# Front of a gated delta-rule layer: squares summed in column tiles, norms one visit later, clip and mask on GpSimd

## What is computed

```python
qkv = jax.nn.silu(_causal_conv1d(qkv, conv_weight))      # 4 taps
...
q = _l2norm(q) * Dk ** (-0.5)                            # x * rsqrt(sum(x * x) + 1e-6)
k = _l2norm(k)
...
g = jnp.cumsum(g.reshape(Bq, H, nc, chunk_size), axis=-1)
decay_mask = jnp.exp(jnp.clip(g[..., :, None] - g[..., None, :], -30.0, 30.0))
decay_mask = decay_mask * jnp.tril(jnp.ones((chunk_size, chunk_size), jnp.float32))
attn = -(jnp.einsum('bhcid,bhcjd->bhcij', k_beta, k) * decay_mask)
attn = jnp.where(upper, 0.0, attn)
...
qk = jnp.einsum('bhid,bhjd->bhij', q_c, k_c)
intra = jnp.where(mask_upper1, 0.0, qk * dm_c)
```

## Time and profile before

| What | Value |
|---|---|
| three runs | 4242.19, 4244.93, 4248.18 us (median 4244.93) |
| profiled execution | 4242.88 us, of it span 4241.1 us |
| mean granted TensorE clock | 0.953 |
| TensorE busy | 3878.7 us, 91% |
| VectorE busy | 2586.0 us, 61% |
| ScalarE busy | 2192.8 us, 52% |
| GpSimd busy | 942.5 us, 22% |
| the stage `delta_front` | about 1383 to 1887 us |

### The profile page before, as it was taken

One profiled execution on the slowest core, in us unless ns is written; L12 is line 12 of the kernel. 1 busy time (PEld: TensorE's weight loads), 2 busy tenths in 40 slices (PEclk: granted clock), 3 DMA queues, 4 the chain that ended last, 5 costly groups with the idle time before them and its releaser, 6 DMA issues. The chain is left out here.

```text
span 4241.1 us, 74265 instructions
## 1 busy us (share of the span) xinstructions
PE 3878.7 (91%) x25346; PEld 2809.3 (66%) x25346; DVE 2586.0 (61%) x7005; ACT 2192.8 (52%) x5801; POOL 942.5 (22%) x849
## 2 busy tenths in 40 slices
PE   7989889899895899979999999999999999978778
PEld 4555545555553666658888888888888888854444
DVE  4753467787523789966666666666666666532632
ACT  3741256676312566655665666666666666632122
POOL 0010010000000344543233323323322323311311
PEclk9999989998996999989999999999999999979879
DMA  2010100000100666553333333333333333222002
GB/s 79 1 35 0 49 1 2 2 2 2 33 0 22 195 229 221 204 195 89 84 84 95 82 91 95 94 81 93 90 78 93 87 82 85 70 81 77 24 28 91
DMA packets 443155, 322.90 MB, mean 76 GB/s; under 512 B 330208, under 2 KB 380064, under 8 KB 440736
## 3 DMA queue, kind: packets, MB, share of 16 engines
q1 hardware_dynamic: 439712, 309.75, 25.4%
q0 software_dynamic: 3072, 8.39, 0.6%
HBM read 200.13 MB, written 117.88 MB: 75 GB/s over the span
## 5 line engine op out<-in xcount | busy, mean ns | idle before, releaser
L2414 ACT ACTIVATE d_heads_VP<-d_heads_chain,d_GALL 128x128 f32<-128x128 f32 x512 | 188.6, 368 | 632.7 <-PE d_heads_chain L2308 629.6
L2557 DVE SCALAR_TENSOR_TENSOR d_heads_S<-d_heads_S,d_GALL,d_heads_chain 128x128 f32<-128x128 f32 x768 | 232.8, 345 | 381.0 <-PE d_heads_chain L2315 379.1
L616 ACT ACTIVATE b_heads_PR<-b_heads_sc,b_heads_NM 128x384 f32<-128x384 f32 (+3 forms) x512 | 272.9, 535 | 161.5 <-DVE b_heads_NM L684 161.5
L2493 POOL TENSOR_TENSOR d_heads_KD<-d_heads_KR,d_GALL 128x512 f32<-128x512 f32 x256 | 269.7, 1074 | 283.9 <-ACT d_heads_KR L2382 283.9
L2194 PE MATMUL d_heads_value<-all_XT,d_heads_WVZ 128*128 128x256 f32 x1024 | 292.5, 389 | 19.2 <-POOL d_heads_ZS L2472 19.2
L2339 PE MATMUL d_heads_projected<-d_heads_WO,d_heads_OT 128*128 128x256 f32 x1024 | 288.4, 394 | 20.1 <-ACT d_heads_OT L2433 19.8
L1981 DVE SCALAR_TENSOR_TENSOR d_front_CY<-d_front_proj,d_CW,d_front_CY 128x511 f32<-128x511 f32 (+2 forms) x384 | 271.8, 744 | 49.8 <-ACT d_front_CY L1892 45.3
L2535 DVE SCALAR_TENSOR_TENSOR d_heads_CY<-d_heads_value,d_CW,d_heads_CY 128x511 f32<-128x511 f32 (+2 forms) x384 | 283.2, 742 | 22.1 <-ACT d_heads_CY L2375 22.0
L2216 PE MATMUL d_heads_value<-d_heads_WVZ,all_XT 128*128 128x256 f32 x1024 | 284.6, 380 | 1.3 <-DVE d_heads_CY L2535 1.3
L2315 PEld LDWEIGHTS d_heads_chain<-d_heads_VP,d_heads_KD 128*128 128x128 f32 x1792 | 264.1, 191 | 29.9 <-ACT d_heads_VP L2414 9.1
L2315 PE MATMUL d_heads_chain<-d_heads_VP,d_heads_KD 128*128 128x128 f32 x1792 | 277.6, 277 | 5.5 <-ACT d_heads_VP L2414 5.5
(11 more groups left out here) (348 smaller groups left out, 8937.3 us busy)
## 6 DMA issues: line engine op xcount, KB each, us to landing
d_kq<-d_front_KQ SPq DMA_DIRECT2D x64, 768.0 KB, 5.0
d_heads_KQ<-d_kq SPq DMA_DIRECT2D x64, 768.0 KB, 4.9
d_heads_GE<-d_gerows SPq DMA_DIRECT2D x128, 256.0 KB, 5.2
d_front_GR<-d_grows SPq DMA_DIRECT2D x32, 512.0 KB, 6.5
d_it<-d_front_LI SPq DMA_DIRECT2D x64, 256.0 KB, 2.1
d_l<-d_front_LI SPq DMA_DIRECT2D x64, 256.0 KB, 3.9
d_heads_ITB<-d_it SPq DMA_DIRECT2D x128, 128.0 KB, 2.9
d_heads_WVZ<-w_d_qkvz SPq DMA_DIRECT2D x32, 256.0 KB, 6.5
```

The costliest lines, as they stand in the source:

```text
L616: nc.scalar.activation(PR[p % 3][j][:, 0:width(p)], SC[p % 2][j][:, 0:width(p)], ACT.Exp, bias=NM[:, u % 2, t, slot:slot + 1], scale=-1.0 ...
L2493: nc.gpsimd.tensor_tensor(KD[i % 2][:, 4 * q:4 * q + 4, h, :], KR[q][:, :, :], decay, ALU.mult).then_inc(kds, 1)
L2557: stt(S[:, h, :], S[:, h, :], gate(i, GEL0 + h, c), R[h][:, HD:2 * HD], ALU.mult, ALU.add).then_inc(su, 1)
```

## The change

- `lengths` is split. `square_rows(i)` makes the column of ones the weights (128x32) and the squares the moving side: four matmuls, for two chunks each, write to four ranges of 32 partitions of SSQ, 256 columns wide. Each row of a range then holds the sums of its two chunks. ScalarE copies this 128x256 block to RW (`copy_rows`), and the new `lengths(i)` turns it with two matmuls: RW's halves as weights, four columns of the identity as the moving side. Both come one visit later than the squares.
- `norms(g - 1)` runs in visit b = 0 of the next group; the root of a group on GpSimd and the store of the scaled products (`store_l`, now b = 2) follow it.
- Clip and mask go from VectorE to GpSimd, as four maxima and four additions a group. `scale` stands between them, `root` behind.
- The scratch tile TMP of the inversion lies in XN, a tile of the whole program.

```diff
-        ones = s.sb("ones", [P, 1])
+        ones = s.sb("ones", [P, HB])
...
+        RW = [s.sb(f"RW{r}", [P, 2, P]) for r in range(2)]
...
-        INV, TO, TMP = s.sb("INV", [P, HB, HB]), s.sb("TO", [P, HB, HB]), s.sb("TMP", [P, HB * HB // 4])
+        INV, TO, TMP = s.sb("INV", [P, HB, HB]), s.sb("TO", [P, HB, HB]), XN[:, 0, :]
...
-                if b == 1 and g >= 1:
+                if b == 2 and g >= 1:
                     store_l(g - 1)
...
+            def square_rows(i):
+                pe.wait_ge(squares, i + 1)
+                if i >= 1:
+                    pe.wait_ge(rowc, i)
+                if i % BATCH == 0 and i > 0:
+                    pe.wait_ge(kss, i)
+                for q in range(4):
+                    mm = nc.tensor.matmul(SSQ[q * HB:(q + 1) * HB, 0:2 * P], ones[:, :],
+                                          SQ[i % 2][:, 2 * q:2 * q + 2, :, :].rearrange("p c k n -> p (c k n)"),
+                                          start=True, stop=True)
+                mm.then_inc(srow, 1)
+
             def lengths(i):
                 g, b = divmod(i, BATCH)
-                pe.wait_ge(squares, i + 1)
-                if b == 0 and g >= 1:
-                    pe.wait_ge(kss, 4 * g)
-                for c in range(NCH):
-                    at = (g % 2) * 32 + b * NCH + c
-                    mm = nc.tensor.matmul(SSQ[:, at:at + 1], SQ[i % 2][:, c, :, :].rearrange("p k n -> p (k n)"),
-                                          ones[:, :], start=True, stop=True)
+                pe.wait_ge(rowc, i + 1)
+                for m in range(2):
+                    at = 2 * P + (g % 2) * 32 + b * NCH + m
+                    mm = nc.tensor.matmul(SSQ[:, at:at + NCH - 1:2], RW[i % 2][:, m, :], C.ident[:, 0:P:HB],
+                                          start=True, stop=True)
                 mm.then_inc(ssq, 1)
...
             for i in range(VISITS):
                 if i + 1 < VISITS:
                     project_keys(i + 1)
+                if i >= 1:
+                    square_rows(i - 1)
                 products(i)
-                lengths(i)
+                if i >= 1:
+                    lengths(i - 1)
+            square_rows(VISITS - 1)
+            lengths(VISITS - 1)
...
+            def copy_rows(i):
+                act.wait_ge(srow, i + 1)
+                if i >= 2:
+                    act.wait_ge(ssq, i - 1)
+                nc.scalar.copy(RW[i % 2][:, :, :], SSQ[:, 0:2 * P].rearrange("p (m n) -> p m n", m=2)).then_inc(rowc, 1)
+
             def exponential(g):
-                act.wait_ge(clips, BATCH * (g + 1))
+                act.wait_ge(hides, BATCH * (g + 1))
...
+                if i >= 1:
+                    copy_rows(i - 1)
                 act.wait_ge(silus, 2 * i + 2)
                 if i >= 2:
-                    act.wait_ge(ssq, i - 1)
+                    act.wait_ge(srow, i - 1)
...
+            copy_rows(VISITS - 1)
...
+            pool.wait_ge(const, 16)
...
+                for b in range(BATCH):
+                    pool.wait_ge(args, BATCH * g + b + 1)
+                    nc.gpsimd.tensor_scalar(D[g % 2][:, b], D[g % 2][:, b], -30.0, None, ALU.max).then_inc(clips, 1)
+
+            def hidden(g):
+                for b in range(BATCH):
+                    pool.wait_ge(clips, BATCH * g + b + 1)
+                    nc.gpsimd.tensor_tensor(D[g % 2][:, b], D[g % 2][:, b], hide[:, :].unsqueeze(1).broadcast_to([P, NCH, CHUNK]),
+                                            ALU.add).then_inc(hides, 1)
...
             exponents(0)
+            hidden(0)
             for g in range(HK):
+                if g + 1 < HK:
+                    exponents(g + 1)
                 if g >= 1:
                     scale(g - 1)
                 if g + 1 < HK:
-                    exponents(g + 1)
+                    hidden(g + 1)
+                if g >= 1:
+                    root(g - 1)
                 if g == 4:
                     pool.wait_ge(invl, 256)
                     nc.gpsimd.memset(INV[:, :, :].rearrange("p a n -> p (a n)")[:, 0:HB * HB:HB + 1], 1.0).then_inc(diag, 1)
-                root(g)
             scale(HK - 1)
+            root(HK - 1)
...
-            def clip(g, b):
-                dve.wait_ge(args, BATCH * g + b + 1)
-                stt(D[g % 2][:, b], D[g % 2][:, b], -30.0, hide[:, :].unsqueeze(1).broadcast_to([P, NCH, CHUNK]),
-                    ALU.max, ALU.add).then_inc(clips, 1)
...
-            for b in range(BATCH):
-                clip(0, b)
             conv(0)
             for i in range(VISITS):
                 g, b = divmod(i, BATCH)
                 if i + 1 < VISITS:
                     conv(i + 1)
                 decayed(i)
-                if b in (1, 2) and g + 1 < HK:
-                    clip(g + 1, 2 * b - 2)
-                    clip(g + 1, 2 * b - 1)
-                if b == 3:
-                    norms(g)
+                if b == 0 and g >= 1:
+                    norms(g - 1)
...
+            norms(HK - 1)
```

12 lines of the change are left out of this document (6 added, 6 removed).

## The result

| | before | changed |
|---|---|---|
| median of 6 runs each, same chip | 4241.85 us | 4231.57 us |
| lowest and highest | 4240.06, 4248.18 | 4225.14, 4233.75 |
| profiled execution (span) | 4242.88 (4241.1) | 4231.71 (4229.9) |

The ratio is 0.997, its 95% interval 0.9957 to 0.9983: faster by 0.3%, 10.3 us, a little more than the 0.2% that can be told from no change.

What follows compares the result with a forecast made beforehand. TensorE was taken as the bound, VectorE close behind, with a ScalarE loop in each fourth visit. Terms -11.2 - 1.5 + 3.5 - 1 = -10.2 us made 4232.7 profiled, 4234.7 as median; forecast 4234, range 4220 to 4254.

Steps and rivals of the forecast that it cites:

- plain groups: Groups without inversion steps, about 8 of 16: TensorE-bound, -1.4 us each with copy and norms wait, -11.2 in all.
- Part 1: Squares on TensorE: 1.80 us a visit becomes 0.69 for column sums plus 0.45 for turning; visit 7.21 to 6.55.
- Parts 2 and 3: ScalarE's new copy adds 0.30 us a group; norms a visit later make TensorE wait about 1.0 us a group.
- Parts 4 and 5: Clips to GpSimd: no steady cost; visits 16 to 45, with inversion steps, become VectorE-bound: -0.2 us a group, -1.5 in all.
- Part 6: Stage start: maxima and additions in series on GpSimd, exponential 5.3 us later; +3.5 us, bounds +2.2 and +7.
- Part 7: Stage end: last norms about 1.2 us later, but GpSimd's root now stands behind the last products; -1 us.
- VectorE binds more than I think: Rival: collisions at the upper bound in all 7.5 middle groups, start +5; no difference, 4243 to 4246; chance 0.29.
- The tiles overlap: Rival denied this: column sums would cost 2.0 us, a group +2.6, about 4288 us; chance 0.07.
- GpSimd as the bound: Rival: slow maxima, over 3 us each, make the exponential wait; at 2 us each about 4250; chance 0.08.
- TensorE as the bound to the end: Rival: norms and copy cost nothing, -2.6 us in each of 16 groups, near 4206 us; chance 0.06.

Runs made afterwards that it cites:

- e8: Changed kernel with the first group's clips on VectorE and each group's norms put back into VectorE's gap under the exponential: 4219.74 us.
- e2: Kernel before with one part of the change alone, clip and mask on GpSimd: 4254.38 us.
- e5: Changed kernel with only the first group's clip and mask back on VectorE, groups 1 to 15 staying on GpSimd: 4218.50 us.

## Why the prediction was right, and where it was off

The forecast was 4234 us, faster; the median is 4231.57, and the difference within the profiled executions -11.2 where the sum said -10.2. The stage alone gives -11.9: +3.5 to the end of group 0 (forecast +2.1), -10.7 in seven plain groups (-9.8), -1.7 in the middle (-1.5) and -3.0 at the end (-1). By its own steps:

**Part 1, sums of squares.** Right in mechanism, a little dear. Sum 0.57 from start to start plus 0.09 at the change of tile form, against 0.69; turning 0.37 against 0.45; a visit 6.43 us against 6.55. I had weighed one pass's length, 0.26 us, for each change of form; the row shows 0.09 more on the projection ahead of the sums and nothing that I can find behind them. The Trainium skill (TensorEngine Tiling (Array Packing), Tiling Modes) says that a change drains the array; the rows agree that it costs something, about a third of that length, once a visit.

**Parts 2 and 3.** The copy out of PSUM takes 0.37 us (0.26 from start to start, I had 0.30). The wait for the norms was put at 1.0 and is 1.00, 12 times.

**Plain groups.** 28.00 us against the 28.4 forecast, -1.84 instead of -1.4 each. Cheaper turnings (3 x 0.08), sums and copy make 0.3 to 0.35 of the 0.44; about 0.1 I can't assign. The eight groups of the sum are 0 to 3 and 12 to 15; group 0 is taken up with the start below. The other seven gained 3.57 + 6.68 + 0.45 = 10.7 us where the sum had 9.8: each group gained more, the wait for a store took 2.0 back, and the last group, which has no group behind it, gained 0.45 only.

**Parts 4 and 5, the clips and the middle.** -1.67 measured in groups 4 to 11, -1.5 forecast, with VectorE as the bound, as said. The loop with long steps has the forecast length: convolutions start at 1617.00, 1639.52 (the fourth) and 1647.40, 30.40 us for the group, where I had 22.6 + 7.9 = 30.5. Counted from E, the end of the second SiLU at 1616.39, it splits as 23.1 + 7.3. What the prediction did not say, and the runs show, is that the clips' part of it was worth nothing: with them on VectorE the middle takes the same time. I had counted the stretch with the clips gone and the collisions in, and never priced it with the clips still there. I also put a collided pair at 0.9 us over its own time; pairs now lose up to 2.0 (1.45 + 1.33 against 0.38 + 0.39). By visit of the group the steps sum to 6.3, 17.4, 4.7 and 10.1 us, where about 5 is undisturbed: two visits carry nearly all of it, the second, and the fourth, which the gap hides. I had 0.9 us in the first visit and 0.9 in the second; measured it is 0.2 and 1.6 a group. That the sum of the two fits is luck: the run without the maxima shifts the meetings and costs 7 us.

The Trainium skill (SBUF – State Buffer, SBUF: two separate sides) states a rule for this: a VectorE operation with two SBUF inputs and a GpSimd operation that reads SBUF take a shared port in turn, each for its whole length. The steps beside subtractions and additions agree: they lose at most about the length of one GpSimd operation (1.45 against 0.37, an addition being 1.31). So do the norms in the gap (e8): slowed with two SBUF inputs, not with one. The root does not: it reads two SBUF tensors for 5.45 us and costs the steps nothing (0.38, 0.39). There the measurement decides, and the best kernel of this study rests on it. That it is this port that they meet at is the Trainium skill's account; the runs show only which operations slow which.

**Part 6, the start: a sum that nearly fits by luck, two wrong terms.** To the end of group 0 the change costs 9.56 - 6.10 = +3.46 us. The forecast to that point is +3.5 for the start and -1.4 for group 0, so +2.1. The start itself, to the second products, is +5.7, inside its bounds of +2.2 and +7, and the rest of group 0 gains 2.2. The **maximum was mis-sized**: 0.61 us by a copy's row, 1.55 measured, outside even the upper bound of 1.09; that is 3.8 us in four, and the additions at 1.23 instead of 1.01 are 0.9 more. So the exponential came 9.6 us late instead of 5.3. The other wrong term is **what TensorE's slow pace does here**: I put it down as a loss of 1 to 2 us. These windows reach from the first products to the second; of before, of the clips alone on GpSimd (e2), of the changed kernel and of the kernel with only the first clips on VectorE (e5):

```profile
1396.75:1408.83 12.08, 12.08 (x41) 8.78 (x41) 6.62 (x10) 4.42 (x6) 0.00 (x0) 0.58 0.81 241
```

```profile
1407.09:1419.86 12.77, 12.77 (x40) 9.40 (x41) 6.77 (x10) 4.42 (x6) 7.55 (x6) 0.54 0.60 172
```

```profile
1413.04:1421.24 8.20, 8.20 (x32) 5.32 (x32) 6.83 (x10) 4.88 (x7) 7.52 (x6) 0.72 0.37 144
```

```profile
1400.62:1408.27 7.65, 7.64 (x32) 4.49 (x32) 6.83 (x10) 4.85 (x7) 7.48 (x6) 0.78 0.70 250
```

Before, TensorE ran products, lengths and most of a projection at 0.50, the 1.2 GHz level (3.25, 3.41 and 5.93 us); now only the products lie there (3.78 us), and the projection behind them takes 4.13. The four kernels say which part of the change did that. With `lengths` the stretch takes 12.08 us, and 12.77 with the exponential late; with the column sums it takes 7.65, and 8.20 with the exponential late. So the new sums are worth 4.4 to 4.6 us in the first visit, more than the 3.1 that I had taken off for the lengths, and the lateness costs 0.6 more. It does not pay for itself, although TensorE stands idle for 9.0 of the 13.7 us at 0.50 in the changed kernel, as in this window of it:

```profile
1404.00:1412.00 8.00, 0.00 (x0) 0.00 (x0) 3.89 (x6) 5.40 (x5) 7.84 (x8) 0.50 0.27 85
```

The kernel with only the first clips on VectorE has the gain without the late exponential, and is 13 us faster than the change: the late start was the part of the change that cost most, and the easiest to avoid.

**Part 7, the end.** Forecast -1, measured -3.0. The order is as forecast: the root stands behind the products of GpSimd (1875.49). It does not hide, though. The last store lands at 1877.56, the root ends at 1880.92 and the next stage begins at 1881.97; before, the stage ended with the last store (1885.96, then 1887.15). From the last of the norms to the next stage it is 10.6 us now and was 12.0, which is 1.4 of the 3.0. The rest is TensorE's pace in the last visit: its products take 2.05 us where they took 3.60, in these windows of before and of the changed kernel:

```profile
1862.00:1874.00 12.00, 10.89 (x69) 9.63 (x67) 7.26 (x12) 5.07 (x6) 0.00 (x0) 0.86 0.73 283
```

```profile
1860.00:1872.00 12.00, 8.12 (x71) 5.80 (x69) 8.86 (x19) 5.92 (x10) 5.17 (x2) 0.99 0.65 251
```

**The rivals.** That VectorE binds more than I think (0.29) is half true: it binds, and a collided pair loses more than I gave it, but fewer pairs collide. The tiles overlap, which the single-tile kernel shows. GpSimd as the bound did not come: busy 333 of 400 us, the exponential waited for it only at the start, though at 1.55 us each the maxima went two thirds of the way from my 0.61 to the 2 us that I had priced. TensorE as the bound to the end (4206) describes neither of the two kernels. The best experiment ends lower than it, with groups of 26.5 to 27.3 us against its 27.2 and without its late start.

## What to carry to other kernels

An operation moved to an idle engine is not free: it costs its latency once where the pipeline fills, and it can lengthen what runs beside it. Before moving work, look for the stretch in which the loaded engine waits each round; here small norms and inversion steps in VectorE's gap, with GpSimd's root beside them, gained 25 us over the kernel with the first clips on VectorE (4218.50 to 4193.87), more than twice what the change itself gained. And order the neighbours: put beside a sensitive operation the one of the other engine that does not slow it.

## What the runs showed of the hardware that was not expected

- GpSimd's maximum with a constant, 128x512, takes 1.49 us (52 in the middle of the stage; 1.55 at the start), slower than a two-input subtraction (1.01) and 2.4 times a copy (0.61). The Trainium skill (GPSIMD Engine Reference, Engine selection) puts one-input operations there at roughly line rate and two-input ones at about twice VectorE's time; this maximum, with one tensor input, is slower than the subtraction with two, while the copy's row alone would not contradict it. Which property of the operation makes it slow stays open.

These are the rows of that middle window, groups by line and form (count, busy us, mean ns of one, idle before):

```profile
L1969 POOL TENSOR_SCALAR d_front_D<-d_front_D 128x512 f32<-128x512 f32 x52 | 77.4, 1488 | 4.2
...
L1974 POOL TENSOR_TENSOR d_front_D<-d_front_D,d_front_hide 128x512 f32<-128x512 f32 x56 | 71.2, 1302 | 0.0
```

- A VectorE product or addition of two tensors in SBUF, 0.37 to 0.41 us alone, takes 0.68 to 1.5 beside GpSimd's subtractions, maxima, products and additions, and its own time beside a GpSimd root of 5.45 us.
- Less work made a section longer: without 32 maxima groups 4 to 11 took 244.0 us instead of 237.1, by other meetings of two engines.
- Four column tiles of 32 took 0.57 us for what one took 1.81, with 0.09 us more on the projection ahead of them for the change of tile form.
